# Last batch placed earlier, fillers dealt to two queues, second list summed one step later

## The reference

```
h   = relu(sage(layernorm(x), W1_l, W1_r, b1));   x2 = x + sage(h, W2_l, W2_r, b2)
      # sage(v) = mean over in-edges of v[src] @ W_l + v @ W_r + b
t   = layernorm(x2)
p   = softmax(t @ router_w.T);  two best experts per node, weights rescaled to sum 1
out = x2 + t + sum over the two chosen experts e of weight * (gelu(t @ w1[e] + b1[e]) @ w2[e] + b2[e])
```

## Time and profile before

| | |
|---|---|
| median of 3 runs | 579.6 us (579.55 to 583.2) |
| the profiled execution | 583.07 us, its span 581.2 us |
| TensorE busy | 551.5 us (95%) |
| VectorE, ScalarE, GpSimd busy | 366.5, 225.1, 184.7 us |
| mean granted clock of TensorE | 0.99 of full speed |

### The profile page before, as it was taken

How to read it: one execution, slowest core, us unless ns; L and a number is a source line. 1 busy time by engine, 2 the same in 40 slices (tenths; PEclk the granted TensorE clock), 3 DMA queues, 4 the chain that set the end, 5 groups by cost and what they waited for, 6 DMA issues and landing times.

```text
span 581.2 us, 11275 instructions
## 1 busy us (share of the span) xinstructions
PE 551.5 (95%) x3023; PEld 332.8 (57%) x3024; DVE 366.5 (63%) x1259; ACT 225.1 (39%) x426; POOL 184.7 (32%) x180
## 2 busy tenths in 40 slices
PE   4999999999999999999989999999999977999993
PEld 2545555555555555555435555555555866888882
DVE  5988677666666766765335667577888763444441
ACT  4666844444443543544100100000003643556553
POOL 3760000000000000000031033433536785787886
PEclk9999999999999999999999999999999997999998
DMA  8521121011110111111472134775335696868774
GB/s 256 153 83 55 56 65 54 29 55 45 37 55 29 54 49 34 55 36 47 81 243 88 51 111 154 242 219 164 129 97 176 145 260 122 138 106 141 130 121 52
DMA packets 64347, 61.29 MB, mean 105 GB/s; under 512 B 11281, under 2 KB 62334, under 8 KB 64302
## 3 DMA queue, kind: packets, MB, share of 16 engines
q1 hardware_dynamic: 48510, 45.92, 26.5%
q0 software_dynamic: 11200, 14.40, 13.3%
q10 hardware_dynamic: 4592, 0.41, 0.6%
HBM read 32.34 MB, written 29.30 MB: 106 GB/s over the span
## 4 chain that ended last, share of the span: by engine, by line
PE 64%; issue 11%; DMA 11%; POOL 5%; DVE 4%; POOLq 4%; ACT 0%; SPq 0%; DVEq 0%; ACTq 0%
PE bank L1514 23%; PE counts_ps L1514 13%; DMA out<-adj 8%; PE bank L1429 8%; PE counts_ps L751 7%; PE bank L1504 7%; POOLq L695 2%; POOL xs_dram L667 2%; DMA y<-y_dram 2%; PE bank L1419 1%; POOLq L700 1%; PE bank L1674 1%; PE bank L1497 1%; POOL out L707 1%; PE bank L1599 1%
## 5 line engine op out<-in xcount | busy, mean ns | idle before, releaser
L1514 PE MATMUL bank<-y,adj 128*128 128x512 f16 x625 | 154.7, 379 | 0.4 <-ACT zt L1751 0.4
L1514 PE MATMUL counts_ps<-y,adj 128*128 128x512 f16 x625 | 144.3, 379 | 1.9 <-DMA y<-y_dram 1.9
L758 ACT ACTIVATE adj<-counts_ps 128x1000 f32 (+1 forms) x80 | 80.2, 1004 | 58.5 <-PE counts_ps L751 58.5
L1514 PEld LDWEIGHTS counts_ps<-y,adj 128*128 128x128 f16 x625 | 60.5, 101 | 64.6 <-DMA y<-y_dram 4.2
L1514 PEld LDWEIGHTS bank<-y,adj 128*128 128x128 f16 x625 | 57.9, 97 | 59.5 <-issue 13.7
L644 POOL IOTA onehots<- 128x8 int32 x1 | 0.1, 142 | 226.9 <-PE counts_ps L751 226.9
L707 POOL DMA_INDIRECT out<-adj x40 | 64.2, 1604 | 15.3 <-issue 7.5
L1661 PE MATMUL counts_ps<-adj 128*128 128x256 f32 x240 | 57.2, 382 | 0.4 <-ACT adj L1873 0.4
L737 DVE TENSOR_TENSOR onehots<-iota,lo_t 125x1024 f16<-125x1024 f16 x80 | 54.8, 685 | 1.7 <-issue 0.9
L751 PEld LDWEIGHTS counts_ps<-onehots 125*128 125x128 f16 x640 | 42.5, 98 | 23.2 <-ACT adj L758 10.8
L1674 PE MATMUL bank<-adj 128*128 x224 | 54.7, 389 | 0.0
(11 more groups left out here) (292 smaller groups left out, 670.3 us busy)
## 6 DMA issues: line engine op xcount, KB each, us to landing
adj<-xs_dram SPq DMA_DIRECT2D x31, 264.0 KB, 3.2
rows<-z_dram SPq DMA_DIRECT2D x49, 128.0 KB, 2.1
z_dram<-zt SPq DMA_DIRECT2D x33, 128.0 KB, 1.7
adj<-in_L_ffn_w SPq DMA_DIRECT2D x16, 256.0 KB, 3.3
rows<-in_x SPq DMA_DIRECT2D x24, 128.0 KB
out<-yo SPq DMA_DIRECT2D x24, 128.0 KB
y_dram<-yo SPq DMA_DIRECT2D x23, 128.0 KB, 1.7
y<-y_dram SPq DMA_DIRECT2D x4, 640.0 KB, 6.8
```

The source lines that it names most:

```text
L758: nc.scalar.activation(adj[:, :, bass.ds(at, GW * WD)].rearrange("p b (h d) -> p b h d", d=WD), counts_ps[:, 2 * (group % 2):2 * (group % ...
L1514: last = te.matmul(to, adj[:, b, t * P:(t + 1) * P], y[:, b, :], start=(b == 0), stop=(b == NT - 1))
```

## The change

Four lists are reordered; no computation is added or left out.

```diff
 # SyncE
             next_rows(5, row_of(5))
-            next_rows(6, row_of(6))
+            row = row_of(6)
+            pad_experts(sp, range(0, 2))
+            next_rows(6, row)
             row = row_of(7)
-            pad_experts(sp, range(0, 3))
+            pad_experts(sp, range(2, 4))
             next_rows(7, row)
-            pad_experts(sp, range(3, NE))
             sp.wait_ge(S["table"], 2)
 # VectorE
             choose_experts(NB - 1)
             shares(NB - 1)
+            place(NB - 1)
             early_weights(4)
             early_result(1)
-            place(NB - 1)
             early_meta(4)
 # TensorE
             for i in range(EARLY):
+                if i == 1:
+                    prefix(NB - 1)
                 result_of(e, i, i % 2)
                 if i + 1 < EARLY:
                     e = expert_of(i + 1)
                 if i == 0:
                     score(NT - 1)
-                if i == 1:
-                    prefix(NB - 1)
+                hidden(i + 2, i % 2)
+                turn_rows((i + 3) % 2, 16 * ((i + 3) // 2 + 1))
                 if i == 4:
                     list_units(spread, bank[0], 2)
-                hidden(i + 2, i % 2)
-                turn_rows((i + 3) % 2, 16 * ((i + 3) // 2 + 1))
 # ScalarE
                     turn_rows(i + 3, (i + 3) % 2)
                     weigh(i, i // UNITS, i % UNITS)
+                if 1 <= i <= 2:
+                    pad_experts(act, range(2 * i + 2, 2 * i + 4))
```

## The result

The changed kernel takes 576.61 us (median of 11 runs, 574.99 to 578.58); the kernel before, run beside it, 581.78 (11 runs, 579.55 to 583.65). The ratio is 0.9918, with an interval of 0.9903 to 0.9933: faster by 4.8 us, between 3.9 and 5.6. The median of 579.6 from which the prediction started was that of three of these runs.

The account below looks back on a forecast made before the run. Fillers on SyncE were taken to delay unit 8's load and so unit 7's addition. Turning unit 8 3.4 earlier plus 2.2 from the held clock gave 5.6 off the median of 579.6: 574.0, range 572.0 to 578.0.

Parts of the forecast that it names:

- rival A: The gain as summed, 5.6, to 574.0; own range 572.5 to 575.3 from ScalarE's price, with held clock; chance 0.52.
- B: Half the gain: clock falls again before unit 8, or never fell in median runs; 576.2 to 577.7; chance 0.22.
- What bounds it: SyncE's fillers hold unit 8's load until 479.22; the addition of unit 7's first half, at 495.78, carries the shift to the end.
- Prefix and place: TensorE waits 1.0 for masks, its work 1.1 later; VectorE's ends at 458.5 and slots at 459.7, each 2.4 earlier.
- Fillers on SyncE: Two free ahead of unit 6's load, two behind it; unit 7 asked for near 466.5, neither gain nor loss.
- Fillers on ScalarE: Each costs 1.3, two per round 3.2 with the next read, against 2.3 of room: TensorE loses 1.2, ends 0 and 2.4.
- List behind the fifth round: TensorE's hole of 2.50 is filled; list summed at 474.4, not 472.26; table whole at 475.0, 1.1 later.
- Unit 8: Load at 475.8, rows turned 3.4 earlier at 479.5; hole of 1.5 keeps the clock, worth 2.2 on TensorE.
- GpSimd: Its additions keep up: unit 7's first half bounded at 490.2 by weighing and 489.9 by its pace; no idle over 1.
- D: Slower through ScalarE: register reads wait for the running activation; at 4.0 per filler, 587; chance 0.06.
- E: More gain: fillers out of the full stretch, so additions land sooner, another 1.5 to 2; 572; chance 0.11.
- C: DMA engines set the landing: unit 8's load asked for earlier but takes as much longer; gain 0 to 1, 579; chance 0.09.

Follow-up runs that it names:

- e1: Kernel before with only the fillers dealt out as in the change; prefix, place and second list stay where they were: 577.75 us, ratio 0.9929 to before.
- e2: Kernel before with only prefix and place of the last batch moved early: 581.38 us, ratio 1.0004 to before.
- e3: Kernel before with only the second list summed behind hidden(6) and the turning of unit 7: 581.3 us, ratio 0.9993 to before.
- e7: Changed kernel with six fillers on SyncE and two on ScalarE, one in each of two rounds: 576.11 us, ratio 0.9895 to the kernel before.
- e6: Changed kernel with the second list summed ahead of hidden(6) again, where it was before: 576.27 us, ratio 0.9898 to the kernel before.
- e4: Kernel before with 19 unused products on TensorE in the hole before unit 8: 583.61 us, ratio 1.0045 to before.
- e9: Kernel before with 10 unused products on TensorE in the hole before unit 8: 580.93 us, ratio 0.9992 to before.
- e11: e7 with the second list ahead of hidden(6) as in e6: 576.79 us, ratio 0.9924 to the kernel before.
- e5: Changed kernel with no filler on ScalarE; SyncE issues the last four behind unit 7's load: 578.63 us, ratio 0.9949 to the kernel before.
- e10: e5 with seven unused products on TensorE in its hole before unit 8: 578.63 us, ratio 0.9945 to the kernel before.
- e8: Changed kernel with each of SyncE's four fillers issued twice, the copy into memory nobody reads: 580.86 us, ratio 0.9980 to the kernel before.
- e12: e11 with three additions of GpSimd, in place of two, ahead of batch 6's scatters: 577.1 us, ratio 0.9931 to the kernel before.

## Why the prediction was right

It forecast 5.6 less than a median of 579.6, so 574.0; measured 576.61, inside the range. Of the 2.6 between them 2.2 is the starting median, of three runs (581.78 with eight more), and 0.4 the sum, 5.6 against 5.2 between the medians (4.8 by the ratio).

How close the number came is in part luck. 576.61 lies outside rival A's own range of 572.5 to 575.3, and inside B's of 576.2 to 577.7, though B's fallen clock didn't come: the starting median put it there. Taken as a gain, 4.8 (3.9 to 5.6) lies in A's range of 4.3 to 7.1, and B's reached to 3.4 only. So the mechanism was A's, though its sum of 5.6 is 1.6 above the 4.0 by which the 15th addition moved.

Point by point, on before's clock:

- **What bounds it.** Right. The fillers ahead of unit 8's load held it, and the 15th addition carries the difference to the end: e1 has most of the gain, e2 and e3 have none, and the time follows that addition in 12 of 13 kernels.
- **Prefix and place.** Right: TensorE waited 0.93 and began it at 457.1; the ends were there at 458.4 (forecast 458.5), with two fillers ahead of unit 6's load. By themselves they bring nothing (e2). With them the first filler is issued at 459.2 (457.96 + 1.22), without them, in e1, at 462.0. What that is worth isn't resolved: e1 has 4.1 of the 4.8, and no run has all fillers on SyncE without early ends.
- **Fillers on SyncE.** Right: unit 7 asked for at 467.2 (forecast 466.5), none behind it.
- **Fillers on ScalarE.** The mis-sized term. Forecast 1.2 on TensorE; it was 0.34 + 1.67 = 2.0, within the ends of 0 and 2.4. A filler was priced at 1.3, with a register read at its median of 0.57. It cost ScalarE 1.1 in the first round (2.2 for two) and 2.1 in the second (4.25 for two), where the reads took 0.97 and 1.41. In e7, with one filler per round, the reads took 0.28 and nothing was lost.
- **List behind the fifth round.** The place was right and the reason for it hollow. It was summed at 475.5 (forecast 474.4), the table was whole at 476.3 (475.0), and unit 8's load issued at 477.6 (475.8). Of the 1.8, 0.8 is ScalarE's, 0.5 the way from the table to the issue (1.3 where I took 0.8), and 0.5 small change of TensorE and VectorE between. From issue to use the load then took 3.45 (479.81 - 476.36) where I took 3.70, so 1.5 of the 1.8 remain. I wrote that TensorE would use the hole; it is late by as much as the hole held, so that ahead of `hidden(6)` the list is 2.9 earlier (e6).
- **Unit 8.** Turned at 481.04, forecast 479.5: a gain of 1.9, not 3.4; this is the largest miss in the sum, and it is the list's and ScalarE's lateness above. The hole before it was 1.82 (forecast 1.5), and the clock held: 0.5 + 1.7 as summed. Unit 7 was weighed 4.1 earlier, not 5.6, and the 15th addition came 4.0 earlier. e4 and e9 measured the clock's 2.2 on TensorE by itself.
- **GpSimd.** Forecast no idle over 1; measured 1.45 before the sixth addition. By the updates of its semaphore in the trace the third addition, issued at 466.32, landed at 472.27: 5.95, against 4.63 before (468.05 to 472.68). The row names ScalarE's weighing instead, but the half that the sixth addition needs was weighed by 466.87, and it starts 0.83 behind the third's landing, as it does in e1, e6, e7 and e11. This wait I hadn't seen. It didn't decide in the changed kernel, where the weighing of unit 7 is later by 0.6, and it decides in e1, e6, e7, e11. A third bound is close in the changed kernel: its 11th addition, at 482.91, waits 0.84 for the weighing of unit 5, and from there the additions follow one another up to the 15th at 490.56, only 0.07 behind unit 7's bound. Both weighings hang on unit 8's load, so this changes nothing in the cause.

Of the rivals, B (the clock falls again) did not happen in the changed kernel, and did in e5, with the same 0.50 at 480 to 482 that it named.

D came near in its cost: a filler of the second round took ScalarE 2.1, against the 2.2 at which D would have used up the table's room in both rounds; the first round's 1.1 kept it away. Its reason, a read that waits until the running activation is done, is not borne out: the read of 1.41 began when ScalarE's last activation had just ended (466.88 and 466.87), and SyncE's reads reached 1.27 in e1. The sign that I had set for B or D, `gelu(4)` or `gelu(5)` over 1.5 behind `hidden`, did appear: `gelu(5)` began 2.35 behind the end of `hidden(5)` (470.55 against 466.23 + 1.97), and neither rival followed, so the sign was set too low. E, additions that land sooner, did not happen; the third took longer.

C's forecast failed: unit 8's rows took 3.45 from issue to use, 3.70 before. Its reason held in a place I had not looked at. I had written that the fillers "leave the full stretch"; they filled the one before (a share of 0.97 in 458 to 470, 0.78 before), and with it the third addition took longer to land. The windows (columns as above) in which it was under way show it, in the kernel before, the changed one, e1 and e5:

```profile
468.00:473.00 5.00, 2.50 (x13) 1.90 (x12) 4.40 (x31) 1.06 (x3) 4.34 (x3) 1.00 1.03 273
```

```profile
466.00:472.00 6.00, 4.13 (x20) 3.36 (x21) 4.69 (x31) 2.20 (x6) 4.74 (x4) 1.00 1.10 316
```

```profile
469.00:475.00 6.00, 3.54 (x18) 2.88 (x19) 4.29 (x31) 1.33 (x3) 4.54 (x3) 1.00 1.05 303
```

```profile
467.00:472.00 5.00, 5.00 (x26) 4.39 (x26) 4.11 (x29) 1.32 (x3) 4.36 (x3) 1.00 1.03 270
```

At 273 and 270 GB/s, with fillers on SyncE alone, the landing took 4.6 and 4.7; at 303 and 316, with ScalarE's beside them, 6.3 and 6.0 (e7: 5.8 at 287). The fillers land more slowly too. Issue to landing of all eight, in the changed kernel and in before:

```profile
DMA to landing us min/median/max: 2.2/4.4/5.3
```

```profile
DMA to landing us min/median/max: 3.5/3.7/3.9
```

The Trainium skill (DMA: Bandwidth & Descriptors, Rules for kernel authors) says that dealing DMAs out over issuing engines saves issue time and brings no bandwidth. The traces agree as far as they go: what was gained was issue order, and transfers beside another queue's took longer, here by 0.7 for a filler at the median and 1.3 for the addition. They don't settle whether a second queue brings bandwidth, since more GB/s were moved beside it, in windows with other transfers in them; and no run parts the second queue from the earlier time of issue.

**Open**: why register reads stretch; why e4 is 2.6 slower where its 15th addition is 1.2 later; and what a held clock is worth at the end, where 2.2 came back on TensorE.

## What to carry over

Where a transfer waits in a queue behind others that could have been issued earlier, the order of issue is worth its full length, but only up to the next bound: write down each bound of the instruction that carries the gain (here two, 0.6 apart, and a third close by) before adding up terms. In this kernel an engine with 1.8 of idle time in each round took one DMA with a register read per round for nothing, and not two. A reordering meant to fill a hole should be tested against leaving it alone, once the other edits have already used that hole up.

## What was unexpected in the hardware

- The register read ahead of a filler varied fivefold within one execution: 0.28 to 1.41 us on ScalarE in the changed kernel. It is no matter of ScalarE alone: SyncE's took 0.26 to 0.68 in the kernel before, but up to 1.27 in e1:

```profile
L437 SPq TENSOR_LOAD <-onehots x4: 275/516/1273, 461.7 to 468.5; - x4
```

- A TensorE hole of 2.50 kept the clock in the profiled execution of the kernel before (the group behind it took 1.97) and lost it in e9's (3.39), with the same instructions ahead of it. In e3 the group behind a hole of 1.48 ran slow (3.17), and in e8 the one behind a hole of 1.93 (2.99), while the changed kernel kept the clock over one of 1.82.
- The same accumulating addition of 128 rows took 4.4 to 5.0 to land with one queue of fillers beside it (before, e2 to e5, e9, e10) and 5.6 to 6.3 with two (changed, e1, e6 to e8, e11). In e12, where it is issued 3.4 us earlier than in e11, it took 4.9 with two.
- An f32 product of 128x256 is recorded as two matmuls and took 0.44 (8.37 / 19 in e4), where I had planned 0.22; the groups of eight in this kernel are four products.
